# A softmax attention over 4096 keys on one core: the two row tiles of the matrix engine get orders of their own

## The chip, the cores and the metric

The kernel runs on one core of one Trainium2 chip, in one launch. The metric is the device time of one execution in microseconds (us). The kernel before takes 1392.46 us (median of three runs, 1392.43 to 1394.41). Its profiled execution took 1394.46 us, of which 1392.7 us lie between the first and the last instruction (the span).

## The reference, cut to what matters

The program is six residual blocks over x (4 batches, 256 rows, 256 columns). The change touches only the first, an attention of x over a context of 4096 rows with 16 heads of width 16:

```python
def xattn0(q, ctx):                      # q = layernorm(x): (4, 256, 256), ctx: (4, 4096, 128)
    qh = (q @ Wq + bq)                   # 16 heads of 16 columns
    kh = (ctx @ Wk + bk)
    vh = (ctx @ Wv + bv)
    scores = qh @ kh.T * 16 ** -0.5      # per head 256 x 4096
    out = softmax(scores) @ vh           # per head 256 x 16
    return concat(out) @ Wo + bo
x = x + xattn0(layernorm(x), ctx)
x = x + attn0(layernorm(x)); x = x + ffn0(layernorm(x))
x = x + xattn1(...); x = x + attn1(...); x = x + ffn1(...)
```

## The kernel before, in words

The 64 pairs of batch and head are worked two heads at a time: 32 groups (`GROUPS`), each of 16 slots (`SLOTS`), so 512 slots `t` (`TOTAL`). A slot scores 256 keys against the 256 queries for both heads of the group. Head 0 lies in partitions 0 to 63 of its operands and head 1 in partitions 64 to 127; a matmul over 64 rows uses one half of TensorE's array, called a row tile here, and the two row tiles can work at the same time. Keys and queries are split into bfloat16 parts, so a score of one head and slot is four matmuls (steps 0 to 3 of `score`, line 541) into one PSUM bank of three that rotate (`HALVES`).

For the softmax each query needs a maximum over all its keys before its group is exponentiated. Two matmuls of 128 queries by 512 keys per slot (`find_max`, line 526) compute leading parts of scores for a group that comes 19 slots later (`LEAD`), alternately on row tile 0 and 1; VectorE takes the maximum of each (`peak`, line 782). Once in a group the maxima are turned into a row of the queries ("turn shift": TensorE at line 697, ScalarE at line 983), and once in a group the finished sums are divided ("normalize": TensorE at line 746, VectorE at lines 863 and 866).

ScalarE exponentiates each score bank (line 895). Every odd slot TensorE first weighs the values of the two slots before with their exponentials (`weigh`, line 588; 16 matmuls over all 128 rows), then does its odd slot, then the even slot. This text calls what lies between two weighings (one odd slot and the even slot behind it) a block.

Work that prepares later groups is spread over the slots by a table (`plan`, line 400). In 192 of the 256 even slots stands a half job ("fill half" makes keys, "make half" makes values): one float32 product, whose first half of the contraction runs on row tile 0 (line 582) and whose second half on row tile 1 (line 586); ScalarE then copies it out of PSUM (lines 940 and 950). From slot 416 on, jobs of the next block of the network ("stream") take the place of half jobs. Jobs that are not half jobs ("turn ctx" at line 660, "turn shift", the stream's) follow an even slot, and come behind the weighing in an odd slot ("normalize").

Maxima, half jobs and all other jobs share four PSUM banks, 4 to 7, in strict rotation (`misc`, line 519): each takes the bank of the fourth user before it, and waits on TensorE until that user's reader (VectorE for a maximum, ScalarE for a half job) has let it go. TensorE, VectorE and ScalarE each run their own list in the order in which it is written; a wait holds up what is behind it on that engine. SyncE's transfers and GpSimd's splitting of keys are started by signals, not by this order.

Names in the diff: `order(t)` gives which head comes first on ScalarE, (0, 1) in an odd slot and (1, 0) in an even one; `self.maxima(t)` are the two maxima of a slot, the first for head 0; `both_scores` is the even or odd slot where there is neither half job nor maximum to put between.

Of the kernel before, what the change touches and what calls it, by code (L numbers as in the profile page):

```python
# [316 lines left out]
HALF_JOBS = "fill half", "make half"  # L317

# [6 lines left out]
class ContextAttention0:  # L325
# [186 lines left out]
    def tensor(self, e, w):  # L512
# [43 lines left out]
        def both_scores(t):  # L556

            early, late = order(t)
            for step in range(4):
                score(t, early, step)  # L560
                score(t, late, step)

# [48 lines left out]
        def even_slot(t, maxima):  # L611
# [16 lines left out]
            half_job(t, 1, *half)  # L628
            score(t, late, 2, 3)

        def odd_slot(t, maxima):

            early, late = order(t)
# [81 lines left out]
        for t in range(FIRST, TOTAL + 3):  # L715
            maxima = self.maxima(t)
            if t < 0 or t >= TOTAL:
                for n in maxima:
                    find_max(n, t)
# [3 lines left out]
            elif t % 2:  # L723
                weigh(t)
                jobs(t)
                odd_slot(t, maxima)
            else:
                even_slot(t, maxima)
                jobs(t)
# [40 lines left out]
    def vector(self, e, w):  # L770
# [107 lines left out]
    def scalar(self, e, w):  # L878
        k = self.k

        def exponentials(t):

            if 0 <= t < TOTAL:
# [9 lines left out]
                for j in order(t):  # L893
                    w.wait_ge(self.scored[j], (t, j))
# [12 lines left out]
        def jobs(t):  # L907
# [2395 lines left out]
```

## Time and profile before

| | us |
|---|---|
| median of three runs | 1392.46 |
| profiled execution | 1394.46 |
| its span | 1392.7 |
| TensorE matmuls busy | 1325.9 (95%) |
| VectorE busy | 1057.2 (76%) |
| ScalarE busy | 951.0 (68%) |
| GpSimd busy | 286.8 (21%) |

Matmuls of the two row tiles overlap, so TensorE's busy time counts a stretch as busy when only one of its tiles works. The mean granted clock of TensorE is 0.986 of full speed. The slots run from about 65 us to about 930 us of the span; the other five blocks of the network follow.

### The profile page before, as it was taken

How to read it: one execution, taken by the hardware profiler on the slowest of the kernel's cores; microseconds unless marked ns; L12 is line 12 of the kernel's file. 1: busy time of each engine (PE TensorE's matmuls, PEld its weight loads, DVE VectorE, ACT ScalarE, POOL GpSimd, SP SyncE). 2: the span in 40 equal slices, each digit the busy share in tenths (PEclk: the TensorE clock that was granted, in tenths of full speed). 3: DMA queues.
4: the chain of work that ended last, by engine and by line, in shares of the span. 5: the costliest groups of instructions: out<-in, count | busy, mean ns of one | idle time of the engine just before them, and what ended most of it. 6: DMA issues, size and time to landing. Idle time of an engine off the chain costs nothing.

```text
span 1392.7 us, 33516 instructions
## 1 busy us (share of the span) xinstructions
PE 1325.9 (95%) x13666; PEld 846.1 (61%) x13666; DVE 1057.2 (76%) x2114; ACT 951.0 (68%) x2027; POOL 286.8 (21%) x321
## 2 busy tenths in 40 slices
PE   7799999999999999999999898889999999989998
PEld 4355555556655555565555555547448999856666
DVE  4777888887888888888888878536877678678757
ACT  5367888888888878888876666654886554448721
POOL 3354223332233223322332000000012100002110
PEclk9899999999999999999999999998989999999999
DMA  5847454365453454543446221021202310356000
GB/s 172 187 140 199 116 128 103 92 142 130 122 141 78 119 136 123 135 106 99 108 96 197 51 52 37 1 62 51 71 24 76 111 57 1 98 134 135 2 1 31
DMA packets 98794, 134.60 MB, mean 97 GB/s; under 512 B 11024, under 2 KB 74128, under 8 KB 92688
## 3 DMA queue, kind: packets, MB, share of 16 engines
q1 hardware_dynamic: 98640, 132.45, 37.8%
q8 instruction: 108, 1.77, 0.6%
q14 instruction: 46, 0.38, 0.1%
HBM read 94.15 MB, written 38.27 MB: 95 GB/s over the span
## 4 chain that ended last, share of the span: by engine, by line
PE 83%; DVE 6%; ACT 6%; DMA 2%; issue 1%; SPq 1%; POOL 1%; ACTq 0%; DVEq 0%
PE psum L605 18%; PE psum L551 17%; PE psum L537 8%; PE psum L2285 4%; PE psum L582 3%; PE psum L586 3%; PE psum L2259 3%; ACT probs L895 2%; PE psum L1379 2%; PE psum L3004 2%; PE psum L1776 1%; PE psum L3014 1%; PE psum L275 1%; PE psum L746 1%; PE psum L660 1%
## 5 line engine op out<-in xcount | busy, mean ns | idle before, releaser
L786 DVE TENSOR_REDUCE peaks<-psum 128x1 f32<-128x512 f32 x1024 | 641.2, 684 | 120.1 <-PE psum L537 118.3
L895 ACT ACTIVATE probs<-psum 128x512 f32<-128x512 f32 x1024 | 539.3, 600 | 170.0 <-PE psum L551 163.6
L551 PE MATMUL psum<-queriesT,keysT 64*128 64x256 bf16 (+1 forms) x4096 | 465.3, 271 | 24.9 <-ACT probs L895 24.9
L551 PEld LDWEIGHTS psum<-queriesT,keysT 64*128 64x128 bf16 (+1 forms) x4096 | 284.4, 95 | 162.1 <-issue 93.6
L537 PE MATMUL psum<-keysT,queriesT 64*128 64x512 bf16 x1024 | 315.9, 383 | 9.4 <-DMA keysT<-key_parts 4.5
L605 PE MATMUL psum<-probs,values 128*17 128x256 f32 x4096 | 273.0, 382 | 0.0
L605 PEld LDWEIGHTS psum<-probs,values 128*17 128x17 f32 x4096 | 100.5, 96 | 111.5 <-ACT probs L895 55.9
L1065 POOL CAST key_parts<-key_f 128x512 bf16<-128x512 f32 x57 | 34.7, 610 | 467.7 <-ACT key_f L940 430.9
L537 PEld LDWEIGHTS psum<-keysT,queriesT 64*128 64x128 bf16 x1024 | 92.9, 93 | 55.9 <-DVE peaks L786 45.9
L2072 ACT ACTIVATE weights<-psum,peaks 128x256 f32<-128x256 f32 x128 | 58.6, 484 | 12.4 <-DVE peaks L1941 12.2
L2285 PEld LDWEIGHTS psum<-ctx_nat,ring 128*128 128x128 f32 x512 | 64.6, 191 | 3.6 <-ACT ring L2420 0.7
L1067 POOL TENSOR_TENSOR key_r<-key_f,key_parts 128x512 f32<-128x512 f32 x57 | 65.8, 1155 | 4.6
L1071 POOL TENSOR_TENSOR key_parts<-key_r,key_parts 128x512 bf16<-128x512 f32 x57 | 65.8, 1155 | 4.6
L2285 PE MATMUL psum<-ctx_nat,ring 128*128 128x129 f32 x512 | 65.9, 275 | 0.7 <-ACT ring L2420 0.6
L2259 PE MATMUL psum<-early_weights,ctx_T 128*128 128x256 f32 x256 | 63.2, 380 | 0.0
L586 PE MATMUL psum<-ctxT,wk 64*128 64x256 f32 x192 | 60.2, 393 | 0.0
L586 PE MATMUL psum<-wv,ctxT 64*128 64x256 f32 x192 | 59.2, 388 | 0.0
L582 PE MATMUL psum<-ctxT,wk 64*128 64x256 f32 x192 | 59.1, 387 | 0.0
L2410 ACT ACTIVATE ring<-psum 128x512 f32<-128x512 f32 x64 | 37.7, 596 | 29.2 <-PE psum L2259 28.9
L582 PE MATMUL psum<-wv,ctxT 64*128 64x256 f32 x192 | 56.6, 374 | 0.0
L2420 ACT ACTIVATE ring<-ring 128x1024 f32<-128x1024 f32 (+1 forms) x36 | 34.6, 961 | 24.3 <-DVE ring L2330 24.1
L1597 POOL TENSOR_TENSOR small<-small,const 128x2 f32<-128x2 f32 x8 | 5.6, 702 | 206.6 <-DVE small L1465 206.5
(325 smaller groups left out, 1919.9 us busy)
## 6 DMA issues: line engine op xcount, KB each, us to landing
keysT<-key_parts SPq DMA_DIRECT2D x186, 256.0 KB, 5.7
key_parts<-key_parts SPq DMA_DIRECT2D x90, 256.0 KB
ctx_nat<-in_ctx_dram SPq DMA_DIRECT2D x32, 256.0 KB, 3.1
ctx_in<-in_ctx_dram SPq DMA_DIRECT2D x24, 256.0 KB, 5.5
ctx_turned<-ctxT SPq DMA_DIRECT2D x24, 256.0 KB, 6.5
ctx_T<-ctx_turned SPq DMA_DIRECT2D x12, 512.0 KB, 4.0
qk_parts<-early_weights SPq DMA_DIRECT2D x24, 128.0 KB
q_parts<-q_parts SPq DMA_DIRECT2D x20, 128.0 KB
```

The costliest lines, as they stand in the source:

```text
L537: e.matmul(ps, self.queriesT[own, MAIN, u % 2, g, qt * P:(qt + 1) * P], self.keysT[own, MAIN, i % RING, c * BANK:(c + 1) * BANK], start=Tr ...
L551: made = e.matmul(ps[:, e2 * S:(e2 + 1) * S], self.keysT[own, plane, i % RING, kt * P:(kt + 1) * P], self.queriesT[own, plane, u % 2, g, : ...
L582: e.matmul(k.ps(name)[:, 0:S], stationary, moving, start=True, stop=False).then_inc(*self.half_made.up((job,) + tuple(a)))
L586: e.matmul(k.ps(name)[:, 0:S], stationary, moving, start=False, stop=True).then_inc(*made_by.up(done))
L605: made = e.matmul(k.bank(SUMS)[32 * quad:32 * quad + DH + 1, 0:S], self.values[b % 2][:, kt, g * GH + j, :], self.probs[:, (SLOTS * i + p) ...
L786: e.tensor_reduce(self.peaks[:, i % 2, j * QT + qt, c:c + 1], k.ps(("max", n)), AX.X, ALU.max).then_inc(*self.peaked.up(n))
L895: e.activation(self.probs[:, t % RINGP, 2 * j * S:(2 * j + 2) * S], k.ps(("scores", t, j)), ACT.Exp).then_inc(*self.exped.up((t, j)))
L1067: e.tensor_tensor(self.key_r[:, :], k_f, part(0), ALU.subtract).then_inc(*w.up(self.split_pool, ("rest",) + key))
L1071: e.tensor_tensor(part(2), self.key_r[:, :], part(1), ALU.subtract).then_inc(*w.up(self.split_pool, ("part2",) + key))
L2072: made = e.activation(self.weights[:, (2 * q + i) % self.NR, kt, :], k.ps(("scores3", q, i))[:, kt * S:(kt + 1) * S], ACT.Exp, bias=self.p ...
L2259: made = e.matmul(ps[:, i * S:(i + 1) * S], l.ctx_T[:, b % 2, kt * P:(kt + 1) * P], l.qcT[:, b * S:(b + 1) * S], start=True, stop=True)
L2285: made = e.matmul(k.ps(("weigh4", b, i))[:, 0:C + 1], self.at(n)[:, column:column + P], l.ctx_nat(b % 2)[:, kt, :], start=(kt == 0), stop= ...
```

## The change

On TensorE the shared orders of the two heads are gone. An odd slot now issues all four steps of head 0, but only steps 0 and 1 of head 1; steps 2 and 3 of head 1 open the next even slot. An even slot holds three maxima (the two of its own slot and the first of the slot after), and the fourth maximum of the block follows the weighing, in the odd slot. The half job's first part opens the even slot and its second part comes behind the first step of head 0. Blocks with and without a half job use the same order. On ScalarE the copy of a half job moves from behind the slot's second exponential to ahead of it. On VectorE the jobs of an odd slot move from ahead of its maxima to behind them, and the maxima are taken in their own order.

```diff
+OTHER_JOBS = ("turn ctx", "fill keys", "split rest", "turn x", "keep queries", "make queries", "split queries", "turn shift",
+              "make values", "stream")
+ALL_JOBS = HALF_JOBS + OTHER_JOBS
...
-        def even_slot(t, maxima):
+        def odd_slot(t):
+
+            ahead = self.maxima(t)
+            score(t, 0, 0)
+            for n in ahead[1:]:
+                find_max(n, t)
+            score(t, 0, 1)
+            score(t, 1, 0)
+            score(t, 0, 2)
+            score(t, 1, 1)
+            score(t, 0, 3)
+
+        def even_slot(t):
 
             halves = [job for job in self.due.get(t, ()) if job[0] in HALF_JOBS]
             w.wait_ge(self.shiftT_kept, t // SLOTS)
             w.wait_ge(self.ones_in, 0)
-            if not halves:
-                both_scores(t)
-                for n in maxima:
-                    find_max(n, t)
-                return
-            half, = halves
-            early, late = order(t)
-            half_job(t, 0, *half)
-            score(t, early, 0, 1, 2, 3)
-            for n in maxima:
+            for half in halves:
+                half_job(t, 0, *half)
+            if t:
+                score(t - 1, 1, 2, 3)
+            score(t, 1, 0, 1, 2)
+            ahead = self.maxima(t)
+            for n in ahead[:1]:
                 find_max(n, t)
-            score(t, late, 0, 1)
-            half_job(t, 1, *half)
-            score(t, late, 2, 3)
-
-        def odd_slot(t, maxima):
-
-            early, late = order(t)
-            if not maxima:
-                both_scores(t)
-                return
-            first = maxima[0]
-            score(t, early, 0)
-            find_max(first + late, t)
-            score(t, early, 1, 2)
-            score(t, late, 0)
-            score(t, early, 3)
-            score(t, late, 1)
-            find_max(first + early, t)
-            score(t, late, 2, 3)
+            score(t, 1, 3)
+            for n in ahead[1:]:
+                find_max(n, t)
+            for n in self.maxima(t + 1)[:1]:
+                find_max(n, t)
+            score(t, 0, 0)
+            for half in halves:
+                half_job(t, 1, *half)
+            score(t, 0, 1, 2, 3)
...
         for t in range(FIRST, TOTAL + 3):
-            if 0 <= t < TOTAL and t % 2:
-                jobs(t)
-                for n in reversed(self.maxima(t)):
-                    peak(n)
-            else:
-                for n in self.maxima(t):
-                    peak(n)
-                jobs(t)
+            for n in self.maxima(t):
+                peak(n)
+            jobs(t)
...
                 for j in order(t):
+                    if t % 2 == 0 and j == 0:
+                        jobs(t, HALF_JOBS)
                     w.wait_ge(self.scored[j], (t, j))
...
             else:
                 exponentials(t)
-                jobs(t)
+                jobs(t, OTHER_JOBS if 0 <= t < TOTAL else ALL_JOBS)
```

TensorE, an even slot with a half job and a turn of the context behind it, in the kernel before (L551 scores, L537 maxima, L582 and L586 the two parts of the half job, L660 the turn, L605 the weighing; in brackets the signals waited for: `peaked` is VectorE's on a maximum, `exped` an exponential's, `v_kept` and `key_kept` ScalarE's copy of a half job):

```order
L582 MATMUL psum<-wv,ctxT 128x256 [waits peaked]
L551 MATMUL psum<-queriesT,keysT 128x256 [waits exped]
L551 MATMUL psum<-queriesT,keysT 128x256 x3
L537 MATMUL psum<-keysT,queriesT 128x512 [waits peaked] x2
L551 MATMUL psum<-queriesT,keysT 128x256 [waits exped]
L551 MATMUL psum<-queriesT,keysT 128x256
L586 MATMUL psum<-wv,ctxT 128x256 [waits half_made]
L551 MATMUL psum<-queriesT,keysT 128x256 x2
L660 MATMUL psum<-const,ctx_in 128x128 [waits ctx0_in,peaked]
L660 MATMUL psum<-const,ctx_in 128x128 x3
L605 MATMUL psum<-probs,values0 17x256 [waits exped]
```

The same even slot on TensorE in the changed kernel (scores are L554 there, maxima L540, the half job L578 and L582, the turn L655):

```order
L578 MATMUL psum<-wv,ctxT 128x256 [waits peaked]
L554 MATMUL psum<-queriesT,keysT 128x256 x2
L554 MATMUL psum<-queriesT,keysT 128x256 [waits exped]
L554 MATMUL psum<-queriesT,keysT 128x256 x2
L540 MATMUL psum<-keysT,queriesT 128x512 [waits peaked]
L554 MATMUL psum<-queriesT,keysT 128x256
L540 MATMUL psum<-keysT,queriesT 128x512 [waits peaked]
L540 MATMUL psum<-keysT,queriesT 128x512 [waits keys0_in,peaked]
L554 MATMUL psum<-queriesT,keysT 128x256 [waits exped]
L582 MATMUL psum<-wv,ctxT 128x256 [waits half_made]
L554 MATMUL psum<-queriesT,keysT 128x256 x3
L655 MATMUL psum<-const,ctx_in 128x128 [waits ctx0_in,v_kept]
```

The third maximum has moved into the even slot. The turn's fourth user before is now the half job of this slot, so that it waits for `v_kept` where it waited for `peaked`.

ScalarE, two blocks of the kernel before, an odd slot's two exponentials first (L895 exponentials; L950 the copy of a half job):

```order
L895 ACTIVATE probs<-psum 128x512 [waits scored1]
L895 ACTIVATE probs<-psum 128x512 [waits scored1,weighed]
L895 ACTIVATE probs<-psum 128x512 [waits scored0]
L950 ACTIVATE values1<-psum 128x16x16 [waits v_made]
L895 ACTIVATE probs<-psum 128x512 [waits scored0]
```

The same stretch on ScalarE in the changed kernel (L888 exponentials, L945 the copy of a half job):

```order
L888 ACTIVATE probs<-psum 128x512 [waits scored1]
L888 ACTIVATE probs<-psum 128x512 [waits scored1,weighed]
L945 ACTIVATE values1<-psum 128x16x16 [waits v_made]
L888 ACTIVATE probs<-psum 128x512 [waits scored0] x2
L888 ACTIVATE probs<-psum 128x512 [waits scored1]
```

The copy has moved by one place, from behind the block's fourth exponential to behind its third.

VectorE at an odd slot with "normalize", in the kernel before (L786 maxima, L863 and L866 the division of the sums):

```order
L786 TENSOR_REDUCE peaks<-psum 128x1 [waits max1_made]
L863 RECIPROCAL recip<-psum 128x4 [waits heads_scaled,gathered]
L866 TENSOR_TENSOR x<-psum,recip 128x32 [waits heads_scaled]
L866 TENSOR_TENSOR x<-psum,recip 128x32
L786 TENSOR_REDUCE peaks<-psum 128x1 [waits max1_made]
L786 TENSOR_REDUCE peaks<-psum 128x1 [waits max0_made] x2
```

The same place on VectorE in the changed kernel (L782 maxima, L854 and L857 the division):

```order
L782 TENSOR_REDUCE peaks<-psum 128x1 [waits max1_made]
L782 TENSOR_REDUCE peaks<-psum 128x1 [waits max0_made]
L782 TENSOR_REDUCE peaks<-psum 128x1 [waits max1_made]
L854 RECIPROCAL recip<-psum 128x4 [waits gathered]
L857 TENSOR_TENSOR x<-psum,recip 128x32 [waits heads_scaled]
L857 TENSOR_TENSOR x<-psum,recip 128x32
L782 TENSOR_REDUCE peaks<-psum 128x1 [waits max0_made]
```

The division has moved behind both maxima of its odd slot, the one made in the even slot before and the one made behind the weighing.

## Rows read from the trace of the kernel before

**Rows 1.** The page, busy time of each engine in the span.
```profile
PE 1325.9 (95%) x13666; PEld 846.1 (61%) x13666; DVE 1057.2 (76%) x2114; ACT 951.0 (68%) x2027; POOL 286.8 (21%) x321
```
**Rows 2.** Busy us by window: PE, PEld, DVE, ACT, POOL; then clock, DMA share, GB/s.
```profile
500.00:600.00 100.00, 100.00 (x1312) 60.23 (x1308) 81.05 (x150) 82.88 (x177) 26.36 (x30) 1.00 0.55 137
```
**Rows 3.** Timeline of a plain block, TensorE matmuls: start us, us long, merged instructions.
```profile
447.86 0.39 PE L537 MATMUL psum<-keysT,queriesT 64*128 64x512 bf16 x1
...
449.28 0.38 PE L551 MATMUL psum<-queriesT,keysT 34*128 34x256 bf16 x2
...
449.50 0.38 PE L586 MATMUL psum<-wv,ctxT 64*128 64x256 f32 x1
...
449.80 1.06 PE L605 MATMUL psum<-probs,values 128*17 128x256 f32 x16
...
450.79 0.28 PE L551 MATMUL psum<-queriesT,keysT 64*128 64x256 bf16 x1
```
**Rows 4.** The same block, weight loads on TensorE, in brackets idle time before, releaser.
```profile
448.75 0.09 PEld L537 LDWEIGHTS psum<-keysT,queriesT 64*128 64x128 bf16 x1
...
448.75 0.09 PEld L551 LDWEIGHTS psum<-queriesT,keysT 34*128 34x128 bf16 x1
...
449.02 0.09 PEld L537 LDWEIGHTS psum<-keysT,queriesT 64*128 64x128 bf16 x1 [0.18 <-DVE peaks L786]
...
449.15 0.09 PEld L551 LDWEIGHTS psum<-queriesT,keysT 64*128 64x128 bf16 x1
```
**Rows 5.** The same block on VectorE and ScalarE.
```profile
448.28 2.48 DVE L786 TENSOR_REDUCE peaks<-psum 128x1 f32<-128x512 f32 x4 [0.45 <-PE psum L537]
...
448.50 2.06 ACT L895 ACTIVATE probs<-psum 128x512 f32<-128x512 f32 x4 [0.52 <-PE psum L551]
```
**Rows 6.** Timeline of a block with a turn of the context behind it.
```profile
501.36 2.07 ACT L895 ACTIVATE probs<-psum 128x512 f32<-128x512 f32 x4 [0.59 <-PE psum L551]
...
502.66 0.42 PEld L660 LDWEIGHTS psum<-const,ctx_in 128*128 128x128 f32 x4 [0.31 <-DVE peaks L786]
...
503.30 0.40 ACT L950 ACTIVATE values<-psum 128x256 f32<-128x256 f32 x1
```
**Rows 7.** Timeline of a turn of the shift and the block behind it.
```profile
405.19 2.10 ACT L895 ACTIVATE probs<-psum 128x512 f32<-128x512 f32 x4 [0.60 <-PE psum L551]
407.19 0.47 ACT L940 ACTIVATE key_f<-psum,bk 128x256 f32<-128x256 f32 x1
```
**Rows 8.** The same stretch, weight loads on TensorE.
```profile
406.54 0.09 PEld L697 LDWEIGHTS psum<-ident_b,shift_b 128*2 128x2 bf16 x4 [0.33 <-DVE peaks L786]
...
408.50 0.18 PEld L582 LDWEIGHTS psum<-ctxT,wk 64*128 64x128 f32 x1 [0.25 <-ACT queriesT L983]
...
409.88 0.56 PEld L605 LDWEIGHTS psum<-probs,values 128*17 128x17 f32 x16 [0.31 <-ACT probs L895]
```
**Rows 9.** Timeline of a block with normalize, TensorE's matmuls.
```profile
417.31 0.39 PE L537 MATMUL psum<-keysT,queriesT 64*128 64x512 bf16 x1
...
419.32 1.05 PE L605 MATMUL psum<-probs,values 128*17 128x256 f32 x15
```
**Rows 10.** The same block on VectorE.
```profile
417.42 0.18 DVE L863 RECIPROCAL recip<-psum 128x4 f32<-128x4 f32 x1 [0.69 <-PE psum L746]
...
417.84 2.47 DVE L786 TENSOR_REDUCE peaks<-psum 128x1 f32<-128x512 f32 x4
```
**Rows 11.** Timeline of a block without a half job, TensorE's matmuls.
```profile
715.05 0.39 PE L537 MATMUL psum<-keysT,queriesT 64*128 64x512 bf16 x1
...
716.35 0.62 PE L551 MATMUL psum<-queriesT,keysT 64*128 64x256 bf16 x7 [0.36 <-ACT probs L895]
...
717.12 0.41 PE L605 MATMUL psum<-probs,values 128*17 128x256 f32 x4
```
**Rows 12.** Matmuls of two lines: count, shortest, median and longest ns, first and last start.
```profile
L660 PE MATMUL psum<-const,ctx_in x96: 272/273/331, 92.2 to 593.0; 128*128 128x128 f32 x96
L746 PE MATMUL psum<-const,outT x128: 277/278/298, 112.6 to 929.3; 128*128 128x34 f32 x128
```

More of the change, by code:

```diff
@@ L554, in score @@
                 made.then_inc(*self.scored[j].up((t, j)))
-        def both_scores(t):
-            early, late = order(t)
-            for step in range(4):
-                score(t, early, step)
-                score(t, late, step)
         def half_job(t, part, job, *a):
@@ L615, in even_slot @@
             w.wait_ge(self.ones_in, 0)
-            if not halves:
-                both_scores(t)
-                for n in maxima:
-                    find_max(n, t)
-                return
-            half, = halves
-            early, late = order(t)
-            half_job(t, 0, *half)
-            score(t, early, 0, 1, 2, 3)
-            for n in maxima:
-                find_max(n, t)
-            score(t, late, 0, 1)
-            half_job(t, 1, *half)
-            score(t, late, 2, 3)
-        def odd_slot(t, maxima):
-            early, late = order(t)
-            if not maxima:
-                both_scores(t)
-                return
-            first = maxima[0]
-            score(t, early, 0)
-            find_max(first + late, t)
-            score(t, early, 1, 2)
-            score(t, late, 0)
-            score(t, early, 3)
-            score(t, late, 1)
-            find_max(first + early, t)
-            score(t, late, 2, 3)
+            for half in halves:
[5 more added lines that the diff above has]
+            for n in ahead[:1]:
+                find_max(n, t)
+            score(t, 1, 3)
[7 more added lines that the diff above has]
+            score(t, 0, 1, 2, 3)
         def jobs(t):
@@ L715, in tensor @@
         for t in range(FIRST, TOTAL + 3):
-            maxima = self.maxima(t)
+            if t == TOTAL:
+                score(t - 1, 1, 2, 3)
             if t < 0 or t >= TOTAL:
-                for n in maxima:
+                for n in self.maxima(t):
                     find_max(n, t)
@@ L725, in tensor @@
                 jobs(t)
-                odd_slot(t, maxima)
+                odd_slot(t)
             else:
-                even_slot(t, maxima)
+                even_slot(t)
                 jobs(t)
@@ L844, in vector @@
         for t in range(FIRST, TOTAL + 3):
-            if 0 <= t < TOTAL and t % 2:
-                jobs(t)
-                for n in reversed(self.maxima(t)):
-                    peak(n)
-            else:
-                for n in self.maxima(t):
-                    peak(n)
-                jobs(t)
+            for n in self.maxima(t):
+                peak(n)
+            jobs(t)
     def scale_heads(self, e, w, i):
@@ L905, in keep_sums, with jobs @@
                 e.activation(self.outT[:, :], k.bank(SUMS)[:, 0:S], ACT.Copy).then_inc(*self.outT_kept.up(i))
-        def jobs(t):
+        def jobs(t, only):
             for job, *a in self.due.get(t, ()):
+                if job not in only:
+                    continue
                 if job == "turn ctx":
@@ L1001, in scalar @@
                 keep_sums(t)
-                jobs(t)
+                jobs(t, ALL_JOBS)
                 exponentials(t)
@@ L1005, in scalar @@
                 exponentials(t)
-                jobs(t)
+                jobs(t, OTHER_JOBS if 0 <= t < TOTAL else ALL_JOBS)
     def pool_chunks(self):
```

## The prediction

> **What bounds the kernel now.** I read the page first: TensorE's matmuls are busy 95% of the span, VectorE 76%, ScalarE 68% [rows 1]. The windows over the slots show the same more sharply, TensorE 100 of 100 us at full clock, VectorE 81, ScalarE 83 [rows 2]. But TensorE has two row tiles, and a stretch in which one idles counts as busy. So I went to the timeline of one block, of the plain kind that repeats: weighing, odd slot, even slot. From its first maximum to the odd slot after it are 2.94 us (447.86 to 450.79), of which the weighing takes the last 0.99 (449.80 to 450.79); the part between, which the change reorders, is 1.95 us [rows 3].
>
> The least that part can be: each row tile has 8 steps of scores, 2 maxima and one half job. Two steps in a row last 0.38 where one lasts about 0.27, so each adds 0.11; a maximum moves twice the columns, 0.22; a pass of a half job's part as many columns in float32, 0.21, and it has two, 0.43. The last pass starts at 449.50 and the weighing at 449.80, so 0.09 pass until the array is free for it [rows 3]. 8 x 0.11 + 2 x 0.22 + 0.43 = 1.75 us a tile, with the 0.09 it is 1.84. The block has 0.11 us of slack. The waits say where: the last maximum of the block waits 0.18 us for VectorE [rows 4]. It takes the bank of the fourth user before it, which is the first maximum behind the weighing. That one starts at 447.86, its peak at 448.28, and the bank is free at 449.02, 0.74 us later [rows 3 to 5]. This chain, 0.42 + 0.74 = 1.16 us after the odd slot's start, then the last maximum (0.22), the half job's second part (0.43) and the drain, makes the 1.95. VectorE and ScalarE have room: four peaks in 2.48 us, four exponentials in 2.06 us of 2.94 [rows 5].
>
> **The plain block after the change: nearly nothing.** The users of the rotating banks in a block, from the weighing on, were max, max, half, max, max. They become max, half, max, max, max. The last maximum of the even slot (now on row tile 0) still takes the bank of the one behind the weighing, and still can't start before +1.16. Behind it on tile 0 come four steps of scores: 1.17 + 0.22 + 4 x 0.11 + 0.09 = 1.92. On tile 1 the half job's second part starts at +1.40 as before, since it stands behind the wait of the first score of head 0 for an exponential (free at 449.15 = +1.30 [rows 4]). So 1.92 or 1.93 against 1.95: 0.02 less, in 97 plain blocks 1.9 us. Bounds: 0.11 less (both tiles always fed) and 0.06 more (below).
>
> **What the rotation now does to the other jobs: dearer.** One more user stands between half job and the end of the even slot. A job behind the even slot took the bank of a maximum of the odd slot, long read; now its fourth user before is the half job of the same slot, and it waits for ScalarE's copy (`v_kept`, `key_kept` in the order above). The weighing and all else on TensorE queue behind that wait.
>
> Turn of the context. ScalarE starts its exponentials at 501.36, one each (503.30 - 501.36) / 4 = 0.485 us; the copy of the half job came behind the fourth and now comes behind the third, at 501.36 + 3 x 0.485 = 502.82. It takes 0.40, and a bank is let go 0.05 after such an instruction (an exponential of 0.60 that starts at 448.50 frees the bank at 449.15 [rows 4, 5]): 503.27. The turn started at 502.66 [rows 6]. So TensorE stands for 0.61 us. Its own 0.3 us wait in that row is the drain of the half job, no bank. There are 96 / 4 = 24 turns [rows 12], 23 of them behind a half job by the table of jobs: 23 x 0.61 = 14.0 us. Moving the copy one place up has kept this from being a whole exponential more. Bounds: 0 if the copy were done, 1.1 if it came fourth.
>
> Turn of the shift. The same: 405.19 + 3 x 0.485 = 406.64, copy of the longer kind 0.47 [rows 7], 0.05, so 407.16 instead of 406.54 [rows 8]: 0.62 us. Something comes back. In the block behind it the half job waited 0.25 us for ScalarE to keep the turned shift, and that block is 409.88 - 406.54 = 3.34 long, 0.40 over a plain one [rows 8, 3]. With TensorE standing 0.62 earlier on, ScalarE has the shift kept before it is wanted (407.16 + some 0.4 for the turn + its two copies, which end by 408.50 - 407.66 = 0.84 after they can start behind the copy of the half job at 407.19 + 0.47 [rows 7, 8], = 408.40; wanted at 407.16 + 0.08 + 0.99 + 0.45 = 408.68), and the first maximum no longer takes the half job's bank. I credit 0.33, since the four small matmuls themselves (0.07) stay. Net 0.29, in 24 of the 32 groups (those with half jobs): 7.0 us.
>
> Normalize. Its bank (the half job's) is free by then. But the block's second maximum now takes its bank, and VectorE, which used to divide first [rows 10], now does so behind the peak of the maximum behind the weighing. That peak starts at +0.42, lasts 0.60 to the next, the division takes 0.42 (417.42 to 417.84 [rows 10]) and some 0.13 until its bank is free: 0.42 + 0.60 + 0.42 + 0.13 = 1.57. Then second and last maximum together, four steps, drain: 1.57 + 0.02 + 0.22 + 0.44 + 0.09 = 2.34, against 419.32 - 417.31 = 2.01 [rows 9]. So 0.33 us, in 128 / 4 = 32 groups [rows 12], 24 of them beside half jobs. In three of these a bias follows the division on VectorE and delayed the peaks; it no longer stands in the chain, and I take 0.2 less there. 21 x 0.33 - 3 x 0.2 = 6.3 us.
>
> **Blocks without a half job.** The timeline shows a stop of 0.36 us for an exponential, then seven steps, and both maxima at the end: 717.12 - 715.05 = 2.07 [rows 11]. With the maxima ahead of the wait, the four steps of head 0 follow it (+1.30, as 716.35): 1.30 + 0.44 + 0.09 = 1.84. 0.22 less. Some 45 such blocks still have maxima; in about 33 of them it holds: -7.3. In the others a stream job on VectorE stands ahead of the peak of the even slot's third maximum, or behind the odd slot's, and its bank or that peak is waited for: I take 0.75 for the two sums with statistics, 0.8 for each of four divisions, 0.5 for three projections, and 0.3 for five normalizes, 1.5 + 3.2 + 1.5 + 1.5 = 7.7. Not one of these is in the trace as a wait; bounds for the whole item are -7 and +12, I take +0.4.
>
> Sum: -1.9 + 14.0 + 7.0 + 6.3 + 0.4 = 25.8 us. 1394.46 + 25.8 = 1420.3 in the profiled execution's terms; this one lay 2.0 over the median, so 1418.3. The startup before slot 0 and all five later blocks of the network keep their order; transfers are not waited for in these blocks.
>
> The Trainium skill (Perfetto Trace Analysis, Optimization Strategy) says that a gap repeating through a stretch of a saturated engine can mean too little PSUM for the next tile to be allocated. The trace agrees: each repeating wait above is for one of four shared banks. By that rule a better order of issue alone wins little here.
>
> **Rivals.**
> *Both tiles packed, and the banks not in the way.* Each block's part falls to 1.84 (0.11 less in 192 blocks, 21 us, and 0.22 in 45 without half job, 10 us), and the late banks cost nothing: 1362; with the last maximum still bound by its bank, -2 - 10 = -12, and back 8 at the shifts: 1373. Place: the wait of the turns for the half job's bank. It decides from the point where the copy ends before TensorE is through, 0.61 us sooner than I reckon. For it: the two tiles' lists are evenly filled now. Against: ScalarE can't copy before the exponentials ahead of it are done, and these follow each other without a gap [rows 6]. 7%.
> The Trainium skill (TensorEngine Tiling (Array Packing), Key Properties) says that different tiles execute weight loads and matmuls in parallel and operate independently. The trace agrees for what is issued (two tiles' starts at one time), but a wait on one tile holds up the other's next instruction, as it does at 449.02.
> *Packed, and the banks in the way:* 25.8 - 21 + 2 = +7, 1399. 5%.
> *The window is too short.* Tile 0's first maximum now stands behind five steps in a row for tile 1. Today a load for tile 0 passes one for tile 1 that is ahead of it in the program (the two at 448.75 [rows 4]), over four steps. If it can't pass five, that maximum starts 0.13 late, and the last one 0.06: 192 x 0.06 = 11 us more, 1430. 9%.
> *The orders don't matter:* both lists are gated by the same chain, and the jobs' waits fall into time that VectorE or ScalarE would have cost anyway: 1392. 4%.
>
> **How the numbers follow.** Forecast 75%, with its own range 1408 to 1428 (the stream's item and 20% on the waits). The range for 8 in 10 reaches to the packed case: 1401 to 1431. A measurement of this kernel can tell 0.2%, 2.8 us, from no change. Slower: 75 + 9 + 5, less a little for small sums, 0.88; same 0.05; faster 0.07.
>
> **What would show it.** Right: the turns of context and shift wait 0.9 us for ScalarE's copy, blocks with them grow by 0.6; the block behind a shift shrinks by 0.3; a plain block stays at 2.91 to 2.94; in blocks with normalize a maximum waits for the division. VectorE's gap splits in two. Wrong: plain blocks under 2.88 or over 2.97, or turns that start where they did; then the sum is off by 97 times the one or 47 times the other.

## The result and the profile after

The changed kernel takes 1425.62 us (median of four runs, 1420.32 to 1431.69) against 1392.45 (four runs, 1391.34 to 1394.41) in the same comparison: 1.0238 times the time before, with a 95% interval of 1.0188 to 1.0288. The forecast was 1418.3, its range 1401 to 1431. The change costs 33 us where 25.8 were forecast; one of the four executions, the longest, lies above the range. The profiled execution took 1429.36 us, span 1427.5.

The page, busy time by engine, which answers to [rows 1]:

```profile
PE 1343.2 (94%) x13666; PEld 887.6 (62%) x13666; DVE 1069.0 (75%) x2114; ACT 949.0 (66%) x2027; POOL 287.3 (20%) x321
```

The same counts of instructions on each engine: nothing was added, and the 35 us of span come from waits and order. The window that answers to [rows 2] (columns as there):

```profile
500.00:600.00 100.00, 93.53 (x1239) 59.97 (x1232) 78.42 (x140) 77.83 (x164) 25.55 (x30) 1.00 0.52 127
```

TensorE, which had no idle time at all in 100 us, now has 6.5. The waits between 67 and 960 us say for whom (waiting engine and line, the one waited for, us in total, times, longest):

```profile
PEld psum L692 <- ACT key_f L935: 19.5, 24, 0.9
PEld psum L655 <- ACT values L945: 18.4, 22, 0.8
PEld psum L540 <- DVE x L857: 17.1, 29, 0.9
PEld psum L540 <- DVE peaks L782: 12.5, 26, 1.5
```

But for one turn of the context in the startup (0.8 us), none of the first three stood in the trace before. The turn of the shift and the turn of the context wait for ScalarE's copy of the half job, and a maximum waits for the division of "normalize".

To see what each is worth I cut both executions at the starts of the weighings and compared the 255 blocks one by one. The last column is the sum over the blocks of a kind; what lies outside the blocks took 535.0 us before and 534.5 after.

| block | how many | before, us | after, us | difference in all |
|---|---|---|---|---|
| half job, plain | 97 | 2.94 | 2.93 | +0.6 |
| half job and turn of the context | 22 (and one in the startup) | 3.53 | 4.14 | +13.9 |
| half job, turn of the shift behind it | 24 | 2.95 (11), 3.01 (13) | 3.65 (11), 3.81 (13) | +18.1 |
| the block behind the shift | 24 | 3.34 | 3.00 | -8.1 |
| half job and normalize | 24 | 3.57 (3 at 4.30) | 3.90 | +5.9 |
| no half job | 63 | 3.06 where plain | 2.84 where plain | +4.9 |

The plain block of the changed kernel on TensorE's matmuls, VectorE and TensorE again, in order of time (answers to [rows 3] and [rows 5]; start us, us long, engine, line, count of merged instructions, in brackets idle time before and releaser):

```profile
465.72 0.39 PE L540 MATMUL psum<-keysT,queriesT 64*128 64x512 bf16 x1
...
466.15 0.69 DVE L782 TENSOR_REDUCE peaks<-psum 128x1 f32<-128x512 f32 x1 [0.17 <-PE psum L540]
...
466.84 0.44 PE L540 MATMUL psum<-keysT,queriesT 64*128 64x512 bf16 x2
...
467.02 1.89 DVE L782 TENSOR_REDUCE peaks<-psum 128x1 f32<-128x512 f32 x3 [0.18 <-PE psum L540]
...
467.65 1.06 PE L601 MATMUL psum<-probs,values 128*17 128x256 f32 x16
```

The maximum behind the weighing starts at 465.72, its peak at 466.15, and the last maximum (the second of the two merged at 466.84) at 466.90, 1.18 after the first. The weighing starts at 467.65, +1.93. VectorE's one gap of 0.45 us is now two of 0.17 and 0.18.

A block with a turn of the context, timeline (answers to [rows 6]):

```profile
520.18 1.57 ACT L888 ACTIVATE probs<-psum 128x512 f32<-128x512 f32 x3 [0.58 <-PE psum L554]
...
521.63 0.40 ACT L945 ACTIVATE values<-psum 128x256 f32<-128x256 f32 x1
...
522.08 0.42 PEld L655 LDWEIGHTS psum<-const,ctx_in 128*128 128x128 f32 x4 [0.84 <-ACT values L945]
```

Three exponentials from 520.18, the copy at 521.63 (+1.45, as 3 x 0.485), 0.40 long, and the turn starts 0.05 behind it.

A block that ends in a turn of the shift, VectorE first, then the weight loads and ScalarE (answers to [rows 7] and [rows 8]):

```profile
420.58 0.18 DVE L788 TENSOR_REDUCE shift<-peaks 128x4 f32<-128x32 f32 x1
...
421.09 3.08 DVE L782 TENSOR_REDUCE peaks<-psum 128x1 f32<-128x512 f32 x5
```

```profile
422.42 0.09 PEld L540 LDWEIGHTS psum<-keysT,queriesT 64*128 64x128 bf16 x1 [0.43 <-DVE peaks L782]
...
423.17 0.47 ACT L935 ACTIVATE key_f<-psum,bk 128x256 f32<-128x256 f32 x1
...
423.69 0.09 PEld L692 LDWEIGHTS psum<-ident_b,shift_b 128*2 128x2 bf16 x4 [0.72 <-ACT key_f L935]
```

The wait for the copy is as forecast. The first line is what I left out: VectorE's three small instructions that form the shift (L788 and two more, until 421.18) stand ahead of the peaks. In the 13 of the 24 blocks that have no turn of the context ahead of them they push the peak of the maximum behind the weighing back, and the last maximum waits 0.43 us on it. The half job's second part stands behind that maximum on TensorE, and the copy behind the half job: both waits add up.

A block with normalize (answers to [rows 10]), VectorE and the wait on TensorE:

```profile
434.54 0.69 DVE L782 TENSOR_REDUCE peaks<-psum 128x1 f32<-128x512 f32 x1 [0.73 <-PE psum L540]
...
435.15 0.17 DVE L854 RECIPROCAL recip<-psum 128x4 f32<-128x4 f32 x1
...
435.35 0.29 DVE L857 TENSOR_TENSOR x<-psum,recip 128x32 f32<-128x32 f32 x2
...
435.69 0.10 PEld L540 LDWEIGHTS psum<-keysT,queriesT 64*128 64x128 bf16 x2 [0.59 <-DVE x L857]
```

The odd slot starts at 434.11; the maxima get going 1.58 us later (forecast: 1.57). Two maxima start together at 435.69, one on each row tile. The first takes the bank of the normalize. The second takes the bank whose peak started at 434.54, and in the plain block such a bank was free 0.74 us behind its peak's start: by that estimate at 435.28. So the wait for one tile's bank held the other tile's maximum back as well.

A block without a half job (answers to [rows 11]), weight loads: the stop for an exponential is 0.20 us, was 0.36, and the maxima are ahead of it. The weighing comes at 745.92, 1.85 us after the odd slot's start at 744.07 (2.07 before):

```profile
745.37 0.33 PEld L554 LDWEIGHTS psum<-queriesT,keysT 64*128 64x128 bf16 x4 [0.20 <-ACT probs L888]
745.92 0.35 PEld L601 LDWEIGHTS psum<-probs,values 128*17 128x17 f32 x12 [0.21 <-ACT probs L888]
```

Some blocks of this kind did worse than I reckoned. In one a job of the stream (sums and statistics of the next layer) holds VectorE until 772.36:

```profile
771.80 0.65 DVE L1460 TENSOR_SCALAR small<-small 128x2 f32<-128x2 f32 x1
772.36 1.87 DVE L782 TENSOR_REDUCE peaks<-psum 128x1 f32<-128x512 f32 x3
...
773.09 0.10 PEld L540 LDWEIGHTS psum<-keysT,queriesT 64*128 64x128 bf16 x2 [1.54 <-DVE peaks L782]
```

The block takes 4.29 us for 3.06: 1.23 more, where 0.75 was forecast. Right behind it this execution has something that the one before has nowhere among its slots, by windows (the number ahead of the last two is the granted clock):

```profile
769.00:774.00 5.00, 3.74 (x43) 1.97 (x46) 4.00 (x9) 1.61 (x4) 3.90 (x4) 1.00 0.94 324
774.00:784.30 10.30, 10.30 (x74) 5.64 (x68) 5.75 (x13) 4.09 (x8) 1.26 (x1) 0.51 1.04 262
```

TensorE, after 1.3 us of matmul idle in 5, runs 10.3 us at the lower of its two clocks, 1.2 GHz (granted clock 0.51 of full speed). More on it below.

### The profile page after: what moved, and what is told of

The parts are those of the page before. It is cut to its first block, busy times and chain, and to the rows that moved or that the text cites. A ratio compares the mean times of both kernels' runs of the same rounds, so it can differ in the third digit from the quotient of the medians.

```text
span 1427.5 us, 33509 instructions
## 1 busy us (share of the span) xinstructions
PE 1343.2 (94%) x13666; PEld 887.6 (62%) x13666; DVE 1069.0 (75%) x2114; ACT 949.0 (66%) x2027; POOL 287.3 (20%) x321
## 4 chain that ended last, share of the span: by engine, by line
PE 78%; DVE 9%; ACT 8%; issue 3%; DMA 1%; SPq 1%; POOL 1%; ACTq 0%; DVEq 0%; POOLq 0%
PE psum L601 17%; PE psum L554 15%; PE psum L540 8%; ACT probs L888 4%; PE psum L2280 4%; PE psum L2254 3%; PE psum L582 2%; DVE peaks L782 2%; PE psum L1374 2%; PE psum L578 2%; PE psum L2999 2%; PE psum L1771 1%; PE psum L3009 1%; PE psum L275 1%; PE psum L742 1%
## 5 line engine op out<-in xcount | busy, mean ns | idle before, releaser
L782 DVE TENSOR_REDUCE peaks<-psum 128x1 f32<-128x512 f32 x1024 | 657.0, 685 | 169.4 <-PE psum L540 166.3
L888 ACT ACTIVATE probs<-psum 128x512 f32<-128x512 f32 x1024 | 555.6, 602 | 193.0 <-PE psum L554 188.6
L554 PE MATMUL psum<-queriesT,keysT 64*128 64x256 bf16 (+1 forms) x4096 | 483.6, 272 | 2.6 <-ACT probs L888 2.5
L554 PEld LDWEIGHTS psum<-queriesT,keysT 64*128 64x128 bf16 (+1 forms) x4096 | 316.5, 95 | 145.6 <-issue 94.2
L540 PE MATMUL psum<-keysT,queriesT 64*128 64x512 bf16 x1024 | 296.5, 387 | 25.7 <-DVE x L857 8.5
L540 PEld LDWEIGHTS psum<-keysT,queriesT 64*128 64x128 bf16 x1024 | 90.9, 93 | 71.7 <-DVE peaks L782 27.0
L582 PE MATMUL psum<-wv,ctxT 64*128 64x256 f32 x192 | 63.7, 412 | 0.0
L582 PE MATMUL psum<-ctxT,wk 64*128 64x256 f32 x192 | 62.5, 405 | 0.0
L578 PE MATMUL psum<-ctxT,wk 64*128 64x256 f32 x192 | 56.8, 375 | 0.0
L578 PE MATMUL psum<-wv,ctxT 64*128 64x256 f32 x192 | 56.8, 375 | 0.0
L935 ACT ACTIVATE key_f<-psum,bk 128x256 f32<-128x256 f32 x96 | 46.4, 483 | 5.9 <-PE psum L582 5.4
```

What stands on the lines that cost most here:

```text
L540: e.matmul(ps, self.queriesT[own, MAIN, u % 2, g, qt * P:(qt + 1) * P], self.keysT[own, MAIN, i % RING, c * BANK:(c + 1) * BANK], start=Tr ...
L554: made = e.matmul(ps[:, e2 * S:(e2 + 1) * S], self.keysT[own, plane, i % RING, kt * P:(kt + 1) * P], self.queriesT[own, plane, u % 2, g, : ...
L578: e.matmul(k.ps(name)[:, 0:S], stationary, moving, start=True, stop=False).then_inc(*self.half_made.up((job,) + tuple(a)))
L582: e.matmul(k.ps(name)[:, 0:S], stationary, moving, start=False, stop=True).then_inc(*made_by.up(done))
L782: e.tensor_reduce(self.peaks[:, i % 2, j * QT + qt, c:c + 1], k.ps(("max", n)), AX.X, ALU.max).then_inc(*self.peaked.up(n))
L888: e.activation(self.probs[:, t % RINGP, 2 * j * S:(2 * j + 2) * S], k.ps(("scores", t, j)), ACT.Exp).then_inc(*self.exped.up((t, j)))
```

## The experiments

All times are medians of their own comparison, each with the kernel before on the same chip (1393.7 to 1396.1 us); the ratios are to that one. Block times come from the one profiled execution of each.

**1. Divide between the peaks.** On VectorE alone, in the changed kernel: an odd slot's jobs stand between its two peaks, so that the division is again ahead of the peak of the maximum behind the weighing.

```diff
-            for n in self.maxima(t):
+            ahead = list(self.maxima(t))
+            first = 1 if 0 <= t < TOTAL and t % 2 else len(ahead)
+            for n in ahead[:first]:
                 peak(n)
             jobs(t)
+            for n in ahead[first:]:
+                peak(n)
```

> The changed kernel with one edit on VectorE: in an odd slot the division of the sums (and any other job of the slot) stands between the two peaks, ahead of the one behind the weighing. If the division's place is what made blocks with normalize dear, its bank is free before the block's second maximum wants it: these 24 blocks fall from 3.90 us to about 3.60 (the last maximum then waits a little for the later peak, 0.10), and the odd-slot jobs of the stream lose their waits too, about 5 us; turns of the context and of the shift stay as they are (4.14, 3.65 to 3.81). In all 10 to 14 us less than the changed kernel, some 1410 us. If the dearness comes from the order on TensorE instead, nothing changes: 1421.

Measured: 1412.86 us, 1.0134 [1.0115, 1.0152]. VectorE and the last maximum of a block with normalize (odd slot's start 435.01):

```profile
435.12 0.18 DVE L858 RECIPROCAL recip<-psum 128x4 f32<-128x4 f32 x1 [0.41 <-PE psum L742]
...
435.54 2.66 DVE L782 TENSOR_REDUCE peaks<-psum 128x1 f32<-128x512 f32 x4
...
436.27 0.09 PEld L540 LDWEIGHTS psum<-keysT,queriesT 64*128 64x128 bf16 x1 [0.16 <-DVE peaks L782]
```

The division now hides in time in which VectorE waited, the maximum waits 0.16 instead of 0.59, and the block goes from 3.90 to 3.58 us in 21 of the 24 (3.57 before the change) and to 4.31 in the three with a bias (4.30 before); and the block with statistics and the two behind it take 13.1 us together where the changed kernel's profiled execution has 17.3, 3.8 of it by the clock (below). The turns are untouched (4.14, 3.75). So the VectorE part of the change costs about 1%, as the ratios of the two kernels to the one before say (1.0238 and 1.0134).

**2. Skip a bank.** In the changed kernel a turn of the context or shift that follows a half job leaves one bank of the rotation out, and so takes that of a maximum.

```diff
             nonlocal turn
+            if job[0] in ("ctx", "shiftT") and 0 <= t < TOTAL and any(due[0] in HALF_JOBS for due in self.due.get(t, ())):
+                turn += 1
```

> The changed kernel with one edit on TensorE: ahead of a turn of the context or of the shift behind a slot with a half job, one bank of the rotation is passed over, so that the turn takes the bank of a maximum and not that of the half job. If the wait for ScalarE's copy is the cost, the turn waits for the peak of the even slot's first maximum only (free at +2.05 against +2.55 after the odd slot's start): 22 blocks with a turn of the context fall from 4.14 to about 3.63, turns of the shift from 3.65 or 3.81 to about 3.1 to 3.3, and the block behind a shift grows from 3.00 by about 0.2, since ScalarE then keeps the shift late again. In all 16 to 20 us less than the changed kernel, some 1403 us. If the stall comes from elsewhere (drain, ScalarE's order as such), 1421.

Measured: 1409.14 us, 1.0088 [1.0066, 1.011]. VectorE and the turn of the context, odd slot's start 510.24:

```profile
511.54 1.29 DVE L784 TENSOR_REDUCE peaks<-psum 128x1 f32<-128x512 f32 x2 [0.18 <-PE psum L542]
...
512.28 0.42 PEld L657 LDWEIGHTS psum<-const,ctx_in 128*128 128x128 f32 x4 [0.33 <-DVE peaks L784]
```

The turn no longer waits for the copy, and its block goes from 4.14 to 3.63, that of the shift from 3.75 to 3.20 on average, while the block behind the shift goes back from 3.00 to 3.32. The 0.10 us that stay over the kernel before are the bank again: the turn takes that of the block's second maximum, whose peak starts at 511.54, and starts 0.74 later. So the two waits for the copy in the sum are shown. What stays at the shift is 0.10 in 11 blocks, this bank again, and 0.30 in the 13 without a turn of the context ahead, where VectorE's three instructions are late as well.

**3. The copy fourth.** The changed kernel with ScalarE's order of before.

```diff
                 for j in order(t):
-                    if t % 2 == 0 and j == 0:
-                        jobs(t, HALF_JOBS)
...
-                jobs(t, OTHER_JOBS if 0 <= t < TOTAL else ALL_JOBS)
+                jobs(t, ALL_JOBS)
```

> The changed kernel with ScalarE's order of before: the copy of a half job again behind the fourth exponential. If turns wait for that copy, each waits one exponential longer (0.49 us): blocks with a turn of the context go from 4.14 to about 4.62, those with a turn of the shift from 3.65 and 3.81 to about 4.15 and 4.3, plain blocks stay at 2.93. 47 x 0.49 = 23 us more than the changed kernel, some 1444 us. If ScalarE's new order were itself a cost (the exponential of head 0 later), the kernel would get faster: below 1415.

Measured: 1474.05 us, 1.0562 [1.0543, 1.058], 30 us over what I expected. The turns grew as said, and by a little more: 4.75 where 4.62 was expected, and 4.26 on average where 4.15 and 4.3 were. Most of the rest came from where I had not looked. ScalarE's copies and the maximum behind the weighing in two plain blocks (the odd slots start at 492.60 and 495.73):

```profile
492.26 0.49 ACT L933 ACTIVATE key_f<-psum,bk 128x256 f32<-128x256 f32 x1
...
492.81 0.39 PE L540 MATMUL psum<-keysT,queriesT 64*128 64x512 bf16 x1
...
495.39 0.41 ACT L943 ACTIVATE values<-psum 128x256 f32<-128x256 f32 x1
...
495.86 0.39 PE L540 MATMUL psum<-keysT,queriesT 64*128 64x512 bf16 x1
```

The maximum behind the weighing is the fourth user after the half job and takes its bank too. With the copy one exponential later it starts 0.21 and 0.13 us late, and all that hangs on its peak with it: 3.10 us for a plain block on average (without the one in the startup), where 2.93 was expected, and 16.5 us over all 97 against the changed kernel. So the copy's move is not only good for the turns: the new order of TensorE can't do without it.

**4. Both.** The edits of 1 and 2 together, to see if they add up.

> The changed kernel with both edits, the bank passed over and the division between the peaks. If the two causes are separate they add: 28 to 32 us less than the changed kernel, about 1391, that is even with the kernel before or up to 3 us under it, with blocks without a half job at 2.84 against 3.06 as its gain. If they share a cause, no more than the better of the two alone, about 1403.

Measured: 1394.25 us, 0.999 [0.9975, 1.0005]. The two account for all of the loss. What is then left of the change, the staggered orders themselves, gains nothing that can be measured: the blocks without a half job win 5.9 us, and the turns lose 2.2 and 4.6, the one block with a turn in the startup 1.2.

**5. The new order where no half job stands, alone.** On the kernel before:

```diff
             if not halves:
-                both_scores(t)
+                early, late = order(t)
+                score(t, early, 0, 1, 2, 3)
                 for n in maxima:
                     find_max(n, t)
+                score(t, late, 0, 1, 2, 3)
                 return
```

> The kernel before, and in the even slots of blocks without a half job one row tile's four score steps, then the maxima, then the other tile's four, as the change has it there; all other blocks as before. My theory: the part of the change that gains is this one alone, and it stands by itself: where no half job stands, the two maxima lie in the time in which TensorE waits for the exponential of head 1, and the plain block of this kind goes from 3.06 to 2.84 us (12 of them, -2.6), those that end with a load of the stream or a shift from 4.28 to 4.16 to 4.34 and from 3.44 to 3.25 (29 and 6, -1 to +1); sum -3 to -9 us, time 1384 to 1390. Rival: the blocks fell only since the row tiles are staggered in their neighbours too; then nothing goes, 1392 to 1395. Half-job blocks should stay at 2.938 either way.

Measured: 1385.66 us, 0.9953 [0.9937, 0.9969]: faster by half a per cent, and the interval leaves out 1. Weight loads of one such block, odd slot's start 715.93:

```profile
717.24 0.33 PEld L551 LDWEIGHTS psum<-queriesT,keysT 64*128 64x128 bf16 x4 [0.19 <-ACT probs L897]
717.78 0.35 PEld L605 LDWEIGHTS psum<-probs,values 128*17 128x17 f32 x12 [0.21 <-ACT probs L897]
```

1.85 us to the weighing, as in the changed kernel: 10 of the 12 plain ones at 2.84, the other two at 3.34 and 3.35. All blocks without a half job together win 8.6 us. The half-job blocks stayed at 2.94. So this gain needs no staggering in the neighbours.

**6. ScalarE's new order alone.** On the kernel before, the copy behind the third exponential (the reverse of the edit of 3).

> The kernel before, with the new order of ScalarE alone: the half job's copy stands behind the third exponential of a block, not behind the fourth. The one instruction of TensorE that could wait for the copy is the first maximum behind a shift's turn (0.07 to 0.09 us in 24 blocks, at most -2 us), and the fourth exponential comes 0.6 us later, for which the steps of the next block of head 1 wait. My theory: ScalarE has that room, so 1390 to 1396, no difference; the turns of the context and the shift stay at 3.53 and 2.99 us. Rival: the later fourth exponential holds the next block's scores back, and the plain block goes from 2.94 to 3.0 or more: 1400 to 1415.

Measured: 1392.88 us, 0.9984 [0.9967, 1.0001]. No difference that can be told; plain block 2.94, both turns as before. ScalarE had the room.

**7. A short peak.** The changed kernel; the half job's second part ahead of head 0's first step, and the peak of the maximum behind the weighing reads half its columns (it leaves out half of those keys).

```diff
-            score(t, 0, 0)
             for half in halves:
                 half_job(t, 1, *half)
-            score(t, 0, 1, 2, 3)
+            score(t, 0, 0, 1, 2, 3)
...
-            e.tensor_reduce(..., k.ps(("max", n)), AX.X, ALU.max)
+            cols = S if j and (n // 2) % 2 == 0 else BANK
+            e.tensor_reduce(..., k.ps(("max", n))[:, 0:cols], AX.X, ALU.max)
```

> The changed kernel, with two edits: the second part of the half job stands ahead of head 0's first score step in place of behind it, and the peak of the maximum behind the weighing reads half of its 512 columns (so one row maximum of four per block leaves out half of its keys). My theory: the plain block of the changed kernel is bound by a ring that the maximum behind the weighing closes (its duration, its peak on VectorE of some 0.7 us, the bank handed to the next maximum, four score steps); a peak shorter by some 0.25 us gives 0.05 to 0.1 us a block until ScalarE's four exponentials bind, and the plain block goes from 2.926 to 2.83 to 2.88: 97 blocks, -5 to -9 us, and the time to 1416 to 1421, while the blocks with a turn stay at 4.14 and 3.75. Rival: ScalarE binds the plain block already (four exponentials and a copy), and the shorter peak moves nothing: 1422 to 1428.

Measured: 1401.95 us, 1.0069 [1.0052, 1.0085]. Matmuls of a plain block:

```profile
458.63 0.39 PE L540 MATMUL psum<-keysT,queriesT 64*128 64x512 bf16 x1
...
459.74 0.39 PE L540 MATMUL psum<-keysT,queriesT 64*128 64x512 bf16 x2
...
460.49 1.06 PE L601 MATMUL psum<-probs,values 128*17 128x256 f32 x16
```

The plain block is 2.85 (1.86 from the odd slot to the weighing), within what I expected, and within 0.02 of the 1.84 that the row tiles need by the sum in the prediction. But the total fell by 24 us, about three times my number, since the short peak stands in more chains than the plain block's: normalize fell from 3.90 to 3.64 (-6.4 us), the shift's two blocks by 0.08 each on average (-3.9), and the blocks without a half job by 8.4 together, 3.8 of it the granted clock, which is taken up below.

**7a. Only the order of 7.** Every peak reads all its columns.

> The changed kernel with one of the two edits of the run before alone: the half job's second part stands ahead of head 0's first score step, and every peak reads its 512 columns. It tells the two edits apart. My theory: the short peak did it all; the bank of the half job's second part is free long before, and the first score step still comes behind the second maximum, so the plain block stays at 2.926 us, the one with the normalize at 3.90, and the time at that of the changed kernel, 1418 to 1428. Rival: the order did it: plain 2.85, normalize 3.64 us, time 1400 to 1406.

Measured: 1423.36 us, 1.0198 [1.0178, 1.0218]; plain 2.93, normalize 3.90, as in the changed kernel. The order is worth nothing that can be told, so all of 7's gain is the peak. That shows the ring (the chain that closes once a block) by its own length: maximum behind the weighing, peak, bank, last maximum, four steps. It is VectorE's duration, and no tile's supply of work, that sets the plain block of the changed kernel.

**8. The two harmless edits together.** 5 and 6 on the kernel before.

> The kernel before with both edits of the two runs on it: the new order in even slots without a half job, and the half job's copy behind the third exponential. My theory: the two do not touch each other, so the time is that of the first edit plus that of the second, 1382 to 1391. Rival: with the copy earlier, the bank of the first maximum is free before the weighing ends but head 1's exponential is later, and the sum is over that of the first edit alone by 3 us or more.

Measured: 1383.79 us, 0.9933 [0.992, 0.9945], the lowest median of all kernels here: 0.7% better than before and about 3% better than the change. Its interval overlaps that of run 5, so that nothing says that the copy's move adds to it.

## Why the prediction was right, and where it was short

The direction and nearly the whole working held: time within the range, forecast 7.3 us short. In the profiled execution the blocks give 35.3 us where the sum says 25.8. Of the 9.5 between them 4.5 are the blocks without a half job, 3.0 the turns of the shift with the block behind, 2.5 the plain blocks and the startup's, and the other two kinds take 0.5 back.

*The plain block* (forecast -0.02 us each): -0.012, and the chain to the last maximum 1.18 us where 1.17 was worked out. Runs 7 and 7a show the cause. Of the kernel before, the terms named for this chain (1.16, 0.22, 0.43 and 0.09) add up to 1.90, not to the 1.94 of its rows; the 0.04 left over stay unexplained. In all the 97 blocks give +0.6, not -1.9: three behind a bias took 0.18 more each, and one in the startup took 5.84 us for 4.65. In it a maximum waits for a copy of ScalarE, which itself waits for GpSimd (columns as in the waits above):

```profile
PEld psum L537 <- ACT key_f L972: 1.3, 1, 1.3
...
PEld psum L540 <- ACT key_f L967: 2.5, 1, 2.5
```

The first row is of the kernel before, the second of the changed one, whose block starts 0.87 us earlier. The block took 6.06 and 5.41 us in runs 5 and 8, whose blocks without a half job ahead of it are shorter as well, and 4.76 in run 6, where they are not. So of the 1.19 us most is what the blocks ahead gained, given back at a copy that comes no earlier (it comes 0.3 us later here). The prediction counts no such wait.

*Turn of the context* (0.61 each): 0.611. Run 2 takes all but 0.10 of it away. *Turn of the shift* (+0.62, -0.33): the return is 0.338, but the cost is 0.70 in 11 of the blocks and 0.80 in the other 13, 18.1 us in place of 14.9. **This is the first mis-sized term:** I counted ScalarE's wait alone. The changed order had also moved VectorE's three small instructions next to the one peak on which the block hangs, and the wait for a peak adds to the wait for the copy, since the half job's second part is behind it.

*Normalize* (21 x 0.33 less 3 x 0.2): 21 x 0.337 less 3 x 0.39 = 5.9 against 6.3. Run 1 removes it. (The maximum that takes this bank is the even slot's second, the block's third; the prediction calls it the block's second.)

*Blocks without a half job* (+0.4, bounds -7 and +12): +4.9 in the profiled execution. The single prices were close: -0.21 for a plain one (forecast 0.22), a division 0.76 (0.8), a projection 0.47 (0.5), but 1.23 for the sum with statistics (0.75) and 1.17 for a normalize behind a division (0.8). **The second mis-sized term** is the granted clock. The three blocks from 769.5 us on take 17.30 us; in run 7a, whose orders on VectorE and ScalarE are the same, they take 13.53, with nearly the same stop in the first (4.13 for 4.29 us) and no fall. The two windows of run 7a:

```profile
769.00:774.00 5.00, 3.90 (x50) 2.01 (x52) 4.27 (x10) 2.05 (x4) 3.47 (x4) 1.00 0.98 305
774.00:784.30 10.30, 10.07 (x108) 6.18 (x97) 7.76 (x17) 5.58 (x11) 1.27 (x1) 1.00 1.04 252
```

Run 1's profiled execution has the stop as well (4.32 us), and no fall; its three blocks take 13.1:

```profile
766.70:771.70 5.00, 3.71 (x44) 1.96 (x45) 3.91 (x9) 1.57 (x3) 4.01 (x4) 1.00 1.02 342
771.70:782.00 10.30, 10.30 (x113) 6.60 (x113) 8.36 (x18) 5.85 (x11) 1.27 (x1) 1.00 1.05 254
```

Run 3's has both, the stop (4.54) and a fall, and its three blocks take 17.55. So 3.8 us of the profiled execution's 35 are clock, and need not come where the stop does. With all of run 7a's blocks the item is +0.2 in place of +4.9, so that the +0.4 of the prediction was near it, in part by luck: its single prices missed by up to 0.5 us, and the misses cancel. The mean granted clock of the four timed runs goes with it: 0.992 and 0.989 at 1420.3 and 1421.9 us, 0.983 and 0.980 at 1429.4 and 1431.7. The two quicker ones are 2.0 and 3.6 us from the forecast. The changed kernel spreads over 11 us where the one before spreads over 3 in the same comparison. This is no sign of the new order: in the comparison with runs 1 to 4 the kernel before spreads over 9 us in 17 executions, from 1391.25 (clock 0.991) to 1400.20 (0.982), while run 7a, with all the waits of the changed kernel, spreads over 2.8 in its four. What makes the clock fall in one execution and not in another stays open.

The Trainium skill (TensorE: Matmul & The Clock Gate, A second HAM failure mode: psum-queue depth-cycling) says that micro-idles of TensorE between groups of matmuls, as its PSUM banks are cycled through, made its clock go back and forth between half and full in one kernel. The trace agrees in kind: the fall comes behind a stop of the matmuls for a bank (1.26 us at 773.09), and it holds for 10.3 us. It also shows that such a stop need not bring it on: runs 1 and 7a have it, without the fall.

*The rivals.* "Packed, and the banks not in the way" is refuted by the waits of 0.8 and 0.9 us. Its price was wrong too: run 4, with the banks mostly out of the way, is at 0.999 of the kernel before, and not at the 1373 that I gave for banks free but the last maximum still bound. That price took the 8 us back at the shifts, which run 2 shows to go with the wait itself (the block behind is at 3.32 there, not at 3.00), and 10 us for the blocks without a half job, where run 4 wins 5.9. "Packed, and the banks in the way" would have put the plain block at 2.83. "The window is too short" would have put the plain block over 2.97; it is 2.93. "The orders don't matter" is refuted by the total.

The prediction takes the wait at 449.02 for one row tile holding up the other. That row doesn't show it: the load behind it, at 449.15, waits for an exponential, as the prediction itself reckons (free at 449.15). The normalize block of the changed kernel shows it (435.69 and 435.28, above).

One step of the prediction holds more than it said: "moving the copy one place up has kept this from being a whole exponential more" priced the copy for turns alone. Run 3 shows that the plain blocks hang on it too, by 0.17 us each.

## What to carry to other kernels

When jobs share banks in strict rotation, an order of issue is also a table of who waits for whom: before moving one user, write down for every user behind it whose bank it takes now, on which engine that reader stands, and what stands ahead of it there (runs 2 and 3 are the two cases). A change of several orders is best priced by kind of block and tried part by part: here one branch of it, by itself, is worth 0.5%, while the whole costs 2.4%. Of a forecast's small items, look first at the instructions on another engine that end up next to the one reader on which the ring turns.

## What the runs showed of the hardware

Two things I had not expected. A peak over 256 in place of 512 columns in one maximum of four took 21 us off the time (run 7a to run 7; 1.3% by the ratios), though VectorE was busy only 75% of the span (1069.0 us, 1002.8 with the short peak): an engine with a quarter of its time free can set the pace through one instruction of 0.69 us. And where a user of a bank waits for a peak, it starts 0.74 us after the peak's start (448.28 to 449.02 before, 511.54 to 512.28 in run 2), while behind ScalarE's copy it starts 0.05 us after the copy's end (521.63 + 0.40 to 522.08), and so in all 46 turns of the changed kernel that wait for one.
